# Layer-norm and item statistics taken from two rows, or two items, read interleaved

## The reference

```python
hidden = gelu(x @ down_W.T + down_b, exact)            # 256 -> 64
hidden = hidden @ expert_W[id].T + expert_b[id] + domain_emb[id]
x1 = layer_norm(hidden @ up_W.T + up_b + x) * ln_gamma + ln_beta      # statistics 1: per token, 256 values
h = layer_norm(x1) * ln_g + ln_b                                      # statistics 2: per token, 256 values
m_t, v_t = h.mean(1), h.var(1)                                        # statistics 3: per item and feature, 64 tokens
h = (h - m_t) * rsqrt(v_t + 1e-8) * gamma[item] + beta[item]
gates, idx = top_k(softmax(h @ router_w), 2)                          # normalised to sum 1
y = sum over the two experts of gate * (relu(h @ w1 + b1) @ w2 + b2)
out = x1 + y
```

## Time and profile before

| What | us |
|---|---|
| median of three runs (684.7 to 686.81) | 686.0 |
| profiled execution: its own time | 682.35 |
| profiled execution: its span | 680.4 |
| dense stage: start to last scatter issue | 0 to 239.1 |
| first expert product starts | 251.8 |
| DVE busy, of the whole span | 420.9 |
| POOL busy, of the whole span | 257.4 |

### The profile page before, as it was taken

One profiled execution on the slowest core, in us unless ns is written; L12 is line 12 of the kernel. 1 busy time (PEld: TensorE's weight loads), 2 busy tenths in 40 slices (PEclk: granted clock), 3 DMA queues, 4 the chain that ended last, 5 costly groups with the idle time before them and its releaser, 6 DMA issues.

```text
span 680.4 us, 16359 instructions
## 1 busy us (share of the span) xinstructions
PE 561.0 (82%) x4520; PEld 481.8 (71%) x4521; DVE 420.9 (62%) x1417; ACT 283.9 (42%) x631; POOL 257.4 (38%) x215
## 2 busy tenths in 40 slices
PE   0978787788623219999999999999999999999990
PEld 0755554566513218888888888888888888888880
DVE  3358988878897706655656656556556565565650
ACT  0326764665555005443533434435334344353330
POOL 4001377768787600323332223223233332223332
PEclk9858877867966559999999999999999999999995
DMA  4235646454435532433334233343342333433321
GB/s 163 82 111 189 199 149 206 141 171 155 162 120 192 175 92 79 59 40 59 50 44 62 39 54 54 40 60 48 45 62 39 54 54 40 61 46 47 46 25 23
DMA packets 84155, 60.20 MB, mean 88 GB/s; under 512 B 56020, under 2 KB 77269, under 8 KB 83989
## 3 DMA queue, kind: packets, MB, share of 16 engines
q1 hardware_dynamic: 68742, 40.13, 21.2%
q0 software_dynamic: 14304, 18.75, 16.6%
q10 hardware_dynamic: 1088, 1.07, 0.5%
HBM read 23.19 MB, written 25.46 MB: 72 GB/s over the span
## 4 chain that ended last, share of the span: by engine, by line
PE 60%; DMA 2%; issue 0%; POOL 0%; DVE 0%; ACT 0%; SPq 0%; POOLq 0%; DVEq 0%
PE banks L1152 30%; PE banks L1168 29%; DMA out<-yg,token 2%; DMA rT<-queues 0%; POOL out L1120 0%; DVE yb L1265 0%; ACT yg L1207 0%; SPq L1095 0%; POOLq L82 0%; POOLq L1126 0%; DVEq L1265 0%; SPq L1097 0%; POOLq L88 0%
## 5 line engine op out<-in xcount | busy, mean ns | idle before, releaser
L1120 POOL DMA_INDIRECT out<-yg,token x78 | 126.6, 1623 | 308.4 <-ACT yg L1207 185.0
L1152 PE MATMUL banks<-rT,w_high 128*128 128x256 f16 x1248 | 208.5, 274 | 23.3 <-DMA rT<-queues 23.3
L1152 PE MATMUL banks<-rT,w_low 128*128 128x256 f16 x624 | 171.0, 274 | 0.0
L1168 PE MATMUL banks<-w_low,hid_high 128*128 x624 | 170.1, 273 | 0.0
L1168 PE MATMUL banks<-w_high,hid_high 128*128 x624 | 170.1, 273 | 0.0
L1168 PE MATMUL banks<-w_high,hid_low 128*128 x624 | 170.1, 273 | 0.0
L1192 ACT ACTIVATE hid<-banks,feat 128x256 f32<-128x256 f32 x312 | 127.3, 474 | 66.6 <-PE banks L1152 59.6
L1152 PEld LDWEIGHTS banks<-rT,w_high 128*128 x1248 | 122.7, 98 | 38.1 <-issue 23.4
L1207 ACT ACTIVATE yg<-yb,gate 128x256 f32<-128x256 f32 x78 | 35.5, 503 | 203.9 <-DVE yb L1265 203.9
L1236 DVE TENSOR_TENSOR hid_low<-hid,hid_high 128x512 f16<-128x512 f32 x156 | 108.3, 695 | 5.3
L1234 DVE CAST hid_high<-hid 128x512 f16<-128x512 f32 x156 | 72.1, 462 | 54.1 <-ACT hid L1192 31.0
(11 more groups left out here) (164 smaller groups left out, 623.6 us busy)
## 6 DMA issues: line engine op xcount, KB each, us to landing
stage<-expert_w SPq DMA_DIRECT2D x32, 512.0 KB, 3.4
xb<-x SPq DMA_DIRECT2D x8, 512.0 KB
out<-rb SPq DMA_DIRECT2D x8, 512.0 KB, 3.2
queues<-pad_row SPq DMA_DIRECT2D x5, 260.0 KB
out<-yg,token POOLq DMA_INDIRECT x78, 3.8
queues<-pad_row ACTq DMA_DIRECT2D x4, 260.0 KB
wnow<-w_low SPq DMA_DIRECT2D x8, 128.0 KB, 3.2
queues<-h_rows,slot POOLq DMA_INDIRECT x64
```

Of the source, the lines that this page charges most:

```text
L1120: nc.gpsimd.indirect_dma_start(out=out, out_offset=bass.IndirectOffsetOnAxis(ap=token[:, i.par, s:s + 1], axis=0), in_=yg[:, i.par, s, :], ...
L1152: last = nc.tensor.matmul(ps_in(c), w[:, at], rT[:, i.par, v, k, :], start=(n == 0), stop=(n == 3 * DC - 1))
L1168: last = nc.tensor.matmul(ps_out(i.par)[:, s, :], v[:, i.par, c, s * P:(s + 1) * P], w[:, at], start=(n == 0), stop=(n == 3 * FC - 1))
```

## The change

`bn_stats` now reads two rows (two tiles of the same partition), or two items, alternately, element by element, so that what it reports for the even places is the first and for the odd places the second. It is called half as often with twice as many elements, and nothing is joined afterwards. The mean is used where it lies; a `tensor_scalar` on DVE divides the summed squares and adds the epsilon, so that POOL's `rstd` keeps the power alone. The item variance is one operation for each half; POOL waits for each half apart. `item_scale` works on both halves at once: three operations in place of six, the first of which waits for both powers. One `cut_low` is put ahead of `norm_shift`.

```diff
+        def per_token(stats, k):
+            return stats[:].rearrange("p n (h s) -> p (n h) s", h=2)[:, :, k]
...
                 def body(i):
...
-                        rstd(s2.g, mv0, mv0_ready, rs0, x1_ready, ve0_ready, rs0_ready)
+                        rstd(s2.g, var0, var0_ready, rs0, x1_ready, rs0_ready)
                     if s4 is not None:
                         scatter(s4, SENDS[:3])
                     if s3 is not None:
-                        pool.wait_ge(var4_ready, s3.g + 1)
+                        wait_apart(pool, select_copied, (aff_ready, s3.g * 3))
                         for c in range(DC):
                             of_c = slice(c * GI, (c + 1) * GI)
-                            nc.gpsimd.tensor_tensor(rsT[:, of_c], var4[:, of_c], minus_half[:, of_c],
+                            pool.wait_ge(varT_ready, s3.g * DC + (c + 1))
+                            nc.gpsimd.tensor_tensor(rsT[:, of_c], varT[:, of_c], minus_half[:, of_c],
                                                     ALU.pow).then_inc(rsT_ready, 1)
...
                 def item_norm(i):
-                    sc.wait_ge(aff_ready[0], (i.g + 1) * 3)
+                    sc.wait_ge(aff_ready, (i.g + 1) * 3)
...
+                def moments(src, stats, st_sem, pairs):
+                    for n in pairs:
+                        V.bn_stats(stats[:, n, :], src[:, 2 * n:2 * n + 2, :].rearrange("p t d -> p d t")).then_inc(st_sem, 1)
+
+                def variance(g, stats, st_sem, var, var_sem, used_sem):
+                    wait_apart(dve, pool_consts, (st_sem, (g + 1) * GT // 2), (used_sem, g))
+                    V.tensor_scalar(var[:], per_token(stats, 2), 1.0 / D, 1e-5, ALU.mult, ALU.add).then_inc(var_sem, 1)
...
-                    for b in range(GI):
-                        last = V.bn_stats(statsT[:, c * GI + b, :], hT[:, c, b * T:(b + 1) * T])
+                    for b in range(GI // 2):
+                        two = hT[:, c, 2 * b * T:2 * (b + 1) * T].rearrange("p (h t) -> p t h", h=2)
+                        last = V.bn_stats(statsT[:, c * GI // 2 + b, :], two)
...
                     if k == 1:
+                        dve.wait_ge(rsT_ready, (i.g + 1) * DC)
+                        wait(dve, h_ready, i.g)
+                        V.tensor_tensor(aff_a[:], both(rsT[:]), gamma, ALU.mult).then_inc(aff_ready, 1)
                     if k == 2:
+                        dve.wait_ge(aff_ready, i.g * 3 + 1)
+                        V.tensor_tensor(aff_c[:], both(mean), aff_a[:], ALU.mult).then_inc(aff_ready, 1)
                     if k == 3:
+                        dve.wait_ge(aff_ready, i.g * 3 + 2)
+                        V.tensor_tensor(aff_c[:], beta, aff_c[:], ALU.subtract).then_inc(aff_ready, 1)
...
-                        moments_parts(ps_u, stats0, st0_ready, rs0_ready, s2.g)
+                        moments(ps_u, stats0, st0_ready, (0, 1))
                     step(s4, place_rows, 1)
+                    step(s4, place_rows, 2)
                     if s2 is not None:
-                        moments(stats0, st0_ready, mv0, mv0_ready, s2.g)
-                    step(s4, place_rows, 2)
+                        variance(s2.g, stats0, st0_ready, var0, var0_ready, rs0_ready)
                     step(s3, item_parts, 0)
                     step(s4, place_rows, 3)
+                    step(s3, item_variance, 0)
                     step(s3, item_parts, 1)
                     step(s2, centre, 0)
-                    step(s3, item_variance, 0)
+                    step(s3, item_variance, 1)
...
                     step(s2, adapter_norm)
-                    step(s3, item_scale, 0, 0)
+                    step(s3, item_scale, 1)
                     if s2 is not None:
                         dve.wait_ge(x1_ready, s2.g + 1)
-                        moments_parts(rb[:, s2.par], stats1, st1_ready, rs1_ready, s2.g, slice(0, 1))
-                    step(s3, item_scale, 0, 1)
+                        wait(dve, n_ready, s2.g)
+                        moments(rb[:, s2.par], stats1, st1_ready, (0,))
+                    step(s3, item_scale, 2)
                     if s2 is not None:
-                        moments_parts(rb[:, s2.par], stats1, st1_ready, rs1_ready, s2.g, slice(1, 2))
-                    step(s3, item_scale, 0, 2)
+                        moments(rb[:, s2.par], stats1, st1_ready, (1,))
+                    step(s3, item_scale, 3)
+                    step(s3, item_norm_rest, False)
...
+                        variance(s2.g, stats1, st1_ready, var1, var1_ready, rs1_ready)
...
                     step(s3, item_norm_rest, True)
+                    if s2 is not None:
+                        cut_low(i, slice(0, 1))
                     step(s2, norm_shift)
-                    cut_low(i, slice(None))
+                    cut_low(i, slice(0 if s2 is None else 1, None))
```

More of the change, by code:

```diff
@@ L453, in _ @@
                 nc.gpsimd.memset(zeros[:], 0.0).then_inc(rows_cleared, 1)
[L455 to L460, removed]
                 SENDS = [(t, k) for t in range(GT) for k in range(2)]
@@ L471, in scatter, with rstd @@
                             in_=h_rows[:, i.par, t, :].bitcast(U32), in_offset=None).then_inc(scattered[i.par], 16)
+                def rstd(g, var, var_sem, rs, used_sem, rs_sem):
+                    wait_apart(pool, select_copied, (var_sem, g + 1), (used_sem, g))
+                    nc.gpsimd.tensor_tensor(rs[:], var[:], minus_half[:, 0:GT], ALU.pow).then_inc(rs_sem, 1)
                 def body(i):
@@ L794, in item_gammas @@
                     link(V.tensor_scalar(gam, gam, 1e-8, None, ALU.add))
[L797 to L806, removed]
+                def moments(src, stats, st_sem, pairs):
[4 more added lines that the diff above has]
+                    V.tensor_scalar(var[:], per_token(stats, 2), 1.0 / D, 1e-5, ALU.mult, ALU.add).then_inc(var_sem, 1)
                 def centre(i, t):
                     if t == 0:
-                        dve.wait_ge(mv0_ready, i.g + 1)
                         wait(dve, x1_stored[i.par], i.half * 16)
                         wait(dve, n_ready, i.g - 1)
-                    V.scalar_tensor_tensor(rb[:, i.par, t, :], ps_u[:, t, :], mv0[:, t, 0:1], g0[:], ALU.subtract,
-                                           ALU.mult).then_inc(centred_ready, 1)
+                    V.scalar_tensor_tensor(rb[:, i.par, t, :], ps_u[:, t, :], per_token(stats0, 1)[:, t:t + 1], g0[:],
+                                           ALU.subtract, ALU.mult).then_inc(centred_ready, 1)
                 def adapter_norm(i):
@@ L833, in item_parts, with item_variance @@
                     last.then_inc(stT_ready, 1)
[L835 to L844 removed]
+                def item_variance(i, c):
+                    of_c = slice(c * GI, (c + 1) * GI)
+                    dve.wait_ge(stT_ready, i.g * DC + (c + 1))
+                    wait(dve, rsT_ready, i.g * DC)
+                    V.tensor_scalar(varT[:, of_c], per_token(statsT, 2)[:, of_c], 1.0 / T, 1e-8, ALU.mult,
+                                    ALU.add).then_inc(varT_ready, 1)
@@ L845, in item_variance, with item_scale, both @@
+                def item_scale(i, k):
+                    mean = per_token(statsT, 1)
+                    gamma = item_gamma[:, :, bass.ds(i.g * GI, GI)]
+                    beta = item_beta[:, :, bass.ds(i.g * GI, GI)]
+                    def both(ap):
+                        return ap.rearrange("p (c b) -> p c b", c=DC)
                     if k == 1:
-                        V.tensor_tensor(mdiff[:], mdiff[:], mdiff[:], ALU.mult).then_inc(item_step, 1)
+                        dve.wait_ge(rsT_ready, (i.g + 1) * DC)
+                        wait(dve, h_ready, i.g)
+                        V.tensor_tensor(aff_a[:], both(rsT[:]), gamma, ALU.mult).then_inc(aff_ready, 1)
@@ L983, in body @@
-                    step(s3, item_scale, 1, 0)
-                    if s2 is not None:
-                        moments(stats1, st1_ready, mv1, mv1_ready, s2.g)
-                    step(s3, item_scale, 1, 1)
-                    step(s3, item_norm_rest, False)
-                    step(s3, item_scale, 1, 2)
+                        variance(s2.g, stats1, st1_ready, var1, var1_ready, rs1_ready)
                     if s1 is not None:
```

66 lines of the change are left out of this document (17 added, 49 removed).

## The result

The change made the kernel slower, as forecast: 696.0 us (694.95 to 696.35, four runs) against 686.4 for the kernel before (684.7 to 687.31, four runs), a ratio of 1.014 with a 95% interval of 1.0111 to 1.0169, or +9.6 us. The forecast was 695. The profiled execution of after took 694.95 us (span 693.0). Where I compare the two traces step by step I speak of 12.6 us, and where I compare kernels, of ratios.

What follows compares the result with a forecast made beforehand. A 20.07 us ring through DVE, POOL, ACT and PE, not DVE's busy time, sets the pace. Terms of -1.7 + 0.35 + 7.5 + 1.84 + 1.4 = +9.4 us on a 686.0 median gave 695, range 689 to 702.

Steps and rivals of the forecast that it cites:

- the sum: Dense stage, change against the profiled execution before: -1.7 + 0.35 + 7.5 + 1.84 + 1.4 = +9.4 us.
- the rival of 673 us: DVE's own time counts: 1.6 us saved in each of 8 iterations, 13 us, giving 673 us; chance 0.10.
- The rival in which it cancels: Room on ACT and PE leaves only DVE's loss: +0.35 us in each of iterations 3 to 7, 687 us; chance 0.08.
- First statistics and `rstd`: Loop iteration, place_rows to POOL's power: power asked for 0.06 us earlier, and epsilon moved to DVE, -0.31 us.
- Item powers: POOL to DVE in a loop iteration: first aff_a now needs both powers, +1.65 us.
- Register waits of POOL: POOL's two new register waits in the loop: +0.2 us in iterations 4 to 7, none elsewhere.
- `item_scale`: DVE's two longer statistics reads between aff_a and last aff_c: ACT's item norm 1.6 instead of 1.04 us after aff_a, +0.56.
- The clock: PE's router products may run at the lower clock after longer idle: up to 1.66 us in four iterations, +6.6, 702; within range.
- Iteration 3: Four cuts make DVE late, not ACT: aff_a 1.28 us later, 0.93 saved from there to the choice, +0.35.
- Iterations 1 and 2: No scatter before POOL's powers: DVE some 2.5 us sooner at iteration 2's choice, capped by PE's router product, -1.7 us.
- Iterations 8 and 9: Last dense iterations: 8 without registers, +1.84 us; 9 without statistics between, second power +1.64, earlier scatters -0.24, +1.4.
- The alternating read: Statistics reads on DVE: no extra cost assumed; rival of 0.33 us more per read of 512, about 705 us, chance 0.22.

Runs made afterwards that it cites:

- the split scale: The changed kernel with item_scale by halves again, half 0 waiting only for the first item power: 685.82 us, ratio 0.9998 to the kernel before.
- the merged scale by itself: The kernel before with only item_scale changed, all three steps over both halves behind both item powers: 700.99 us, ratio 1.0207.

## Why the prediction was right, point by point

**The total.** The mechanism forecast is the one that the rows show, but that 695 and 696.0 agree within 1 us is in part luck. Trace against trace the dense stage grew by 12.64 us where the sum said 9.4. The medians came out 3 us closer together because the forecast carried over the 3.65 us between before's profiled execution and its median, and after's lies only 1 us below its own.

**What bounds the kernel.** Right, and shown from both sides. With DVE 13.1 us less busy the kernel was slower; without the wait for the second power it was as before (0.9998); with POOL's powers ahead of the scatters instead it was faster (0.9823). The condition named for the rival of 673 us, both powers there when DVE arrives, holds in that variant's trace but for iteration 9 (2.48 us of wait). That its 676 lies near 673 is luck all the same: the rival put 1.6 us in each of eight iterations, and the gain over before stands in three. In iterations 3 and 8, with four cuts, DVE came to the choice without a wait; in 4 it stood 1.08 us before the choice and 0.62 before `low`, and its saved time showed hardly at all. The rival in which it cancels fell too: it took 0.35 us for each of the iterations 3 to 7, and they grew by 1.50 to 3.06. One reading was loose: DVE's slices 5 to 13 hold two sevens beside the eights and nines, so it was 70 to 90% busy and more there.

**First statistics and `rstd`.** -0.06 and -0.31 were forecast, -0.01 and -0.31 measured. The two reads of 512 took 1.20 us to the start of what follows (107.66 to 108.86), 1.22 forecast. From `place_rows` 2 to the variance it is 0.29 us (109.10 to 109.39) where the forecast had 0.11, and this eats the gain: the variance starts 1.92 us after the place (107.47 to 109.39), and before had its aggregate at 1.70 (107.17 to 108.87).

**Item powers.** The largest term and the right one. +1.65 was forecast, +1.41 measured: the pair of powers took 3.28 us in after where the forecast took over before's 3.48, and `aff_a` followed it 0.15 us behind. That the split scale takes the loss away and the merged scale by itself makes it (+14.7) shows the cause.

**Register waits of POOL.** +0.2 was forecast, and there is nothing: in POOL's rows the item powers start 0.02 us after the third scatter ends (113.88 + 1.01 = 114.89), and the second power follows without a gap.

**`item_scale`.** +0.56 forecast and measured, and 0.88 of the 1.60 goes with the reads moved behind, worth 4.7 us by the ratios. The step behind it, item norm to router product, got 0.26 shorter, which the forecast left at nothing.

**The clock.** Not in the sum, but in the range. In iteration 4 it is +0.76 (router product 2.61 instead of 1.92 us, then the transposes back). Products of iterations 3 to 7 took 9.85 us in before's trace and 16.07 in after's, 6.2 more; of these the four of 4 to 7 have 4.6, against the bound of 6.6 that the forecast gave for four. What keeping PE busy gave back by the ratios, some 2 us, is less; the 6.2 holds for the two profiled executions and is not shown for the medians.

**Iteration 3.** This is the term that was furthest off: +0.35 forecast, +1.50 measured. There I had let only DVE's work count from `aff_a` to the choice, and nothing behind the choice. But the router product took 3.58 us after 5.12 idle, where before has

```profile
99.43 1.95 PE L579 MATMUL banks<-rw,hT 128*128 128x8 f32 x16 [0.20 <-ACT hT L672]
```

and what hangs on PE came late on ACT and DVE of after:

```profile
103.49 0.37 DVE L885 MAX8 top<-lg 128x8 f32<-128x8 f32 x4 [0.67 <-ACT lg L680]
...
105.06 1.02 ACT L687 ACTIVATE h_rows<-banks 128x1024 f16<-128x1024 f32 x1 [1.60 <-PE banks L586]
...
106.12 1.22 DVE L910 TENSOR_TENSOR h_rows<-banks,h_rows 128x1024 f16<-128x1024 f32 x1 [0.88 <-issue]
```

`aff_a` comes 0.86 us later after the place (1.28 forecast). From it to the choice 0.34 is saved (8.24 us for 8.58) and not 0.93, since DVE waits 0.67 for the logits. From the choice to the next place 0.98 is lost (3.98 for 3.00), since DVE waits 0.88 before `low` for ACT's `high`. The sum is 1.50.

**Iterations 1 and 2.** -1.7 forecast, -1.20 measured: the gain was capped where I had put the cap, at PE's router product without idle ahead of it, but this began at 79.53, not 79.09.

**Iterations 8 and 9.** +1.84 and +1.4 forecast, +1.66 and +1.30 measured; the same excess of the second power.

**The alternating read.** "Nothing" was taken and is shown. The Trainium skill's full rate for a one-source operation that alternates between two regions ("Vector Engine (DVE) Microarchitecture Reference", Measured stream behaviour on trn2) agrees with the 685 and 696 ns here against 688 and 689 for plain reads; its 1.73 ns a column, for a two-source operation with a hop on every element, does not carry over to this instruction.

**The checks named.** DVE -13 us: 13.1. The wait at `aff_a` 30: 26.4. Item norm 1.6 after `aff_a`: 1.60. A loop iteration about 22: 22.24. A read of 512 at 0.69 us: 0.69.

**What stays open.** Why before's profiled execution was 4 us faster than its median: whether its router products at 1.92 to 2.08 us were luck in that one execution can't be told from one trace. The granted clocks of 31 other executions of the same kernel point that way without proving it: the five fastest (682.28 to 683.71 us) had means of 0.888 to 0.896, the other 26 of 0.879 to 0.889, and the profiled one, 682.35 us, had 0.891. With it stays open how much of 9.6 us is the clock. Nor is it settled why a product ran at the full clock after 3.00 us idle in one trace and at half after 3.15 in another; the idle time just ahead of it does not decide alone, for in the trace of the split scale one took 3.58 us after only 2.30 idle (iteration 4, at 121.49).

## What to carry to other kernels

An engine that is 80% busy isn't the bound if it waits in every iteration for a result it needs next: follow one iteration from a step to the same step through all engines' queues, and price an edit only by what it does on that ring. Fewer, wider operations save the engine's time but join their waits: the joined operation waits for the last of its inputs, and here giving that wait back was worth 10 us, while the change without the join ran level with the kernel before (0.9998) for all the work it saves on DVE. Once the producer was moved ahead in its own queue, the changed kernel ran 10 us under the kernel before; the same move without the change ran 3 to 4 us over it.

## What the runs showed of the hardware

- A `bn_stats` over two rows interleaved costs as much as over contiguous data, in PSUM (685 against 688 ns for 512 elements) and in SBUF (696 against 689; items, 128 elements, 282 against 280). The plain figures are those of the kernel with plain reads.
- POOL's power took 1.04 us for 4 numbers a partition, 1.64 for 8 (3.28 / 2) and 2.94 for 16, each in rows of iteration 4. My estimate from these: about 0.16 us for each further number ((2.94 - 1.04) / 12) on some 0.4 fixed. In before's iteration 4 the pair of 8 took 3.48.
- A router product took 3.58 us (granted clock 0.50) after 3.15 to 5.12 us of idle PE in some iterations, and 2.61 after 2.02, where the trace of before has 1.92 after 3.08. In iterations 8 and 9, after 15.21 and 12.82 us of idle, it took 3.58 in both. Idle transposes ahead of it raised the mean clock over iterations 4 to 9 from 0.68 to 0.77.
